# The last mixing of a four-stream layer: which engine multiplies and adds tile 4, and in which order the output is stored

## The chip, the cores and the metric

The kernel runs on one core of a Trainium2 chip. The metric is the device time of one execution in microseconds. The core has five engines with instruction queues of their own: TensorE (PE in the profile), VectorE (DVE), ScalarE (ACT), GpSimd (POOL) and SyncE (SP), which issues the DMAs of interest here.

## The reference

The whole program is a stack of four layers, each a gated cross attention and a gated feed-forward block on x of shape 4 x 256 x 512 (1024 rows of 512 numbers). The change is in the very last step, the end of the fourth feed-forward block. There a row is seen as four streams of 128 numbers, and `hn`, the normalised row, is mixed by a 4 x 4 matrix of that row:

```python
    H_res = sinkhorn_log(H_res_logits)
    H_pre = jax.nn.softmax(H_pre_logits, axis=-1)
    H_post = jax.nn.softmax(H_post_logits, axis=-1)
    H_res = (1.0 - g) * I + g * H_res
    x_pre = jnp.einsum('btnc,btn->btc', x_streams, H_pre)
    y = x_pre @ W_branch
    x_mixed = jnp.einsum('btij,btjc->btic', H_res, x_streams)
    y_distributed = jnp.einsum('btc,btn->btnc', y, H_post)
    return (x_mixed + y_distributed).reshape(B, T, nC)
```

The block's result, times tanh of a gate, is added to x, and x is the output. The kernel has put the gate into the weights, so that the last step is: X[stream i] += sum over j of H[i, j] * hn[stream j], for every row.

## The kernel before, in words

The 1024 rows are 8 tiles of 128 rows (one row per partition). X lies in SBUF as 8 tiles of 128 x 512, `hn_of(7, t)` is tile t of the normalised rows (in the buffer AR), and H (K3, also in AR) holds 16 weights per row.

Each engine has its program written out by hand, in order, and waits on semaphores (`F3[...]`). The end runs as follows.

- GpSimd (`pool_f3`) forms x_pre, and then spreads y over the streams: for each of the eight tiles one 128x512 multiply into a temporary (`PTMP`) and one 128x512 add into X (`add_spread`, L2465 and L2468). Then it raises "posted". It has nothing more to do.
- VectorE (`dve_f3`) runs the balancing of the matrices in 24 and then 25 linear steps of small operations (L2668, L2675, L2679) that read the kernel matrices KP and KT from PSUM. Then come three small operations that finish H (L2697, L2700, L2704), and "mixed" is raised.
- The mixing itself is split three ways. Tiles 0 to 3: VectorE does 16 multiply-adds of 128x128 per tile (L2718), 64 in all, in two halves (tiles 0 and 1, tiles 2 and 3); within a half the streams j are the outer loop, with a drain between them. After each half it raises "done".
- Tiles 4 to 7: products are written to the buffer R16, and TensorE sums X and the four products of a tile in a PSUM bank with an identity matrix as weights (L2511 for X, L2517 for products). ScalarE copies the bank back to X (L2560) and raises "done_act". The products of tiles 5, 6 and 7 are made by ScalarE, 16 activations of 128x128 per tile (L2566). Those of tile 4 are made by VectorE, four operations of 128x512 (L2708), ahead of its multiply-adds.
- SyncE stores one tile per DMA of 256 KB (L2753) in the order 4, 5, 0, 1, 6, 7, 2, 3. Before each it waits for the semaphore of its tile, and it issues nothing past a wait that isn't met. Then it waits for all stores, and the program ends.

Of the kernel before, what the change touches and what calls it, by code (L numbers as in the profile page):

```python
# [9 lines left out]
ALU = mybir.AluOpType  # L10
# [3 lines left out]
P = 128  # L14
B, S, D = 4, 256, 512
SK = 64
T = B * S // P
# [18 lines left out]
NS = 4  # L36
# [21 lines left out]
def build(nc, x_d, ctxT_d, ctxB_d, gx_d, gf_d, wkv_d, w0q_d, w3q_d, wo_d, w4_d, sc4_d, ze4_d, l1wqv_d, l1kr_d, l1o_d,  # L58
# [3 lines left out]
    with ctx:  # L62
# [10 lines left out]
        X = sb("X", [P, T, D])  # L73
# [15 lines left out]
        rms = sb("rms", [P, T])  # L89
# [22 lines left out]
        def bank(i, n=1):  # L112
            return PS[:, i, :] if n == 1 else PS[:, i:i + n, :].rearrange("p a b -> p (a b)")
# [10 lines left out]
        class Sems:  # L124
# [5 lines left out]
            def __getitem__(self, n):  # L130
# [10 lines left out]
        A2 = Sems("a2", "k_in q_in b_in k_mm keys_ready m_mm turned_copied s_mm shifted exps probs t_mm "  # L141
                        "pt_ready mm acc")
        F2 = Sems("f2", "in0 in1 scaled t_mm whi wlo g_mm u_mm silu act ahi alo mm acc")
        F3 = Sems("f3", "w_in rms gate_exp lg_mm to_act from_act pre preT_mm preT y_mm y_sb post posted mixed prod prod_act "
                        "sum_mm done done_act scaled_half")


# [6 lines left out]
        def hn_of(n, t):  # L154
            if n == 7:
                return AR[:, t * D:(t + 1) * D]
            return HN[:, t % 2, :]
# [1193 lines left out]
        def pe_logits(pe, t):  # L1351
            pe.wait_ge(hi_ready, T * 7 + t + 1)
            if t == 0:
                pe.wait_ge(F3["w_in"], 32)
                pe.wait_ge(A3["piece_lo"], 2 * NU0)
# [1077 lines left out]
        NM = NS * NS  # L2433
        LG = at3(4096, T * NL)
        Z = at3(4352, T * NM)
        K3 = at3(4480, T * NM)
# [10 lines left out]
        PTMP = at3(7424, D)  # L2447
# [2 lines left out]
        KT = bank(6)[:, T * NM:2 * T * NM]  # L2450
        TH = T // 2
        T_DVE = 4
        PE_TILES = range(T_DVE, T)

        def products(t, j):
            at = 4096 + (t - T_DVE) * NS * D + j * D
            return R16[:, at:at + D]

        def pool_f3(pool):
            pool_norm(pool, 7)  # L2460
            tmp = PTMP.rearrange("p (i c) -> p i c", i=NS)

            def add_spread(t, src, weights):

                nc.gpsimd.tensor_tensor(tmp, src.unsqueeze(1).to_broadcast([P, NS, P]),  # L2465
                                        weights.unsqueeze(2).to_broadcast([P, NS, P]), ALU.mult)
                pool.drain()
                nc.gpsimd.tensor_tensor(X[:, t, :], X[:, t, :], PTMP, ALU.add)  # L2468
            pool.wait_ge(F3["post"], 1)
            P3 = PP.rearrange("p (t n) -> p t n", t=T)  # L2470

            H4 = AR[:, 0:T * D].rearrange("p (t n c) -> p t n c", t=T, n=NS)
            for n in range(NS):
                dst = XP if n == 0 else XTMP
                nc.gpsimd.tensor_tensor(dst.rearrange("p (t c) -> p t c", t=T), H4[:, :, n, :],
                                        P3[:, :, n].unsqueeze(2).to_broadcast([P, T, P]), ALU.mult)
                pool.drain()
                if n:
                    nc.gpsimd.tensor_tensor(XP, XP, XTMP, ALU.add)
                    pool.drain()  # L2480
            pool.drain().then_inc(F3["pre"], 1)
            nc.gpsimd.tensor_tensor(PP, PP, tg[:, 1, 3:4].to_broadcast([P, T * 2 * NS]), ALU.mult)
            pool.drain()
            pool.wait_ge(F3["y_sb"], 1)
            for t in range(T):
                add_spread(t, Y[:, t * P:(t + 1) * P], P3[:, t, NS:2 * NS])
                pool.drain()
            pool.drain().then_inc(F3["posted"], 1)

        def pe_f3(pe):  # L2490
            for c in range(C):
                i = nc.tensor.matmul(bank(4)[:, 0:NL], ones[:], W24[:, c * NL:(c + 1) * NL], start=c == 0, stop=c == C - 1)
            i.then_inc(F3["lg_mm"], 1)
            pe_logits(pe, 3)
            pe_turn7(pe, 6)
            pe_logits(pe, 4)
            pe_turn7(pe, 7)
            for t in range(5, T):
                pe_logits(pe, t)
            pe.wait_ge(F3["pre"], 1)  # L2500
            for t in range(T):
                i = nc.tensor.transpose(bank(2, 2)[:, t * P:(t + 1) * P], XP[:, t * P:(t + 1) * P], ident[:])
            i.then_inc(F3["preT_mm"], 1)
            pe.wait_ge(F3["preT"], 1)
            for t in range(T):
                i = nc.tensor.matmul(bank(4, 2)[:, t * P:(t + 1) * P], PT[:, t * P:(t + 1) * P], WB,
                                     start=True, stop=True)
            i.then_inc(F3["y_mm"], 1)
            pe.wait_ge(F3["posted"], 1)
            for k, t in enumerate(PE_TILES):  # L2510
                nc.tensor.matmul(bank(k), ident[:], X[:, t, :], start=True, stop=False)  # L2511
                for j in range(NS):
                    if k == 0:
                        pe.wait_ge(F3["prod"], j + 1)
                    else:
                        pe.wait_ge(F3["prod_act"], NS * (k - 1) + j + 1)
                    i = nc.tensor.matmul(bank(k), ident[:], products(t, j), start=False, stop=j == NS - 1)  # L2517
                i.then_inc(F3["sum_mm"], 1)

        def act_f3(act):  # L2520
            act_norm(act, 7, (6, 7))
            asked = [0]

            def asked_for():
                asked[0] += 1
                act.wait_ge(F3["to_act"], asked[0])

            def run(out, in_, f):
                nc.scalar.activation(out, in_, f).then_inc(F3["from_act"], 1)

            def kernel_matrices():
                Z4 = Z.rearrange("p (t i j) -> p t i j", t=T, i=NS)
                run(KP, Z, ACT.Exp)
                run(KT.rearrange("p (t j i) -> p t j i", t=T, j=NS), Z4.rearrange("p t i j -> p t j i"), ACT.Exp)
            asked_for()
            run(K3, Z, ACT.Exp)
            asked_for()
            run(PP, PP, ACT.Exp)
            asked_for()
            run(MX[:, 0:T * NS], MX[:, 0:T * NS], ACT.Ln)  # L2540
            asked_for()
            run(K3, Z, ACT.Exp)
            asked_for()
            run(MX[:, 0:T * NS], MX[:, 0:T * NS], ACT.Ln)
            asked_for()
            kernel_matrices()
            act.wait_ge(F3["preT_mm"], 1)
            nc.scalar.copy(PT[:], bank(2, 2)).then_inc(F3["preT"], 1)
            act.wait_ge(F3["y_mm"], 1)
            nc.scalar.copy(Y, bank(4, 2)).then_inc(F3["y_sb"], 1)  # L2550
            asked_for()
            run(AR[:, 4800:4864], AR[:, 4800:4864], ACT.Ln)
            asked_for()
            kernel_matrices()
            act.wait_ge(F3["mixed"], 1)
            H3 = K3.rearrange("p (t n) -> p t n", t=T)

            def mixed_tile(k):
                act.wait_ge(F3["sum_mm"], k + 1)
                nc.scalar.copy(X[:, T_DVE + k, :], bank(k)).then_inc(F3["done_act"], 1)  # L2560
            for k, t in enumerate(PE_TILES):
                if k == 0:
                    continue
                for j in range(NS):
                    for i_ in range(NS):
                        i = nc.scalar.activation(products(t, j)[:, i_ * P:(i_ + 1) * P],  # L2566
                                                 hn_of(7, t)[:, j * P:(j + 1) * P], ACT.Copy,
                                                 scale=H3[:, t, i_ * NS + j:i_ * NS + j + 1])
                    i.then_inc(F3["prod_act"], 1)
                mixed_tile(k - 1)  # L2570
            mixed_tile(len(PE_TILES) - 1)

        def dve_f3(dve):
# [128 lines left out]
            H3 = K3.rearrange("p (t n) -> p t n", t=T)  # L2702
            diag = H3[:, :, 0:NM:NS + 1]
            nc.vector.tensor_scalar(diag, diag, SG[:, 2:3], None, ALU.add)  # L2704
            dve.drain().then_inc(F3["mixed"], 1)
            t = PE_TILES[0]
            for j in range(NS):
                nc.vector.tensor_tensor(products(t, j).rearrange("p (i c) -> p i c", i=NS),  # L2708
                                        hn_of(7, t)[:, j * P:(j + 1) * P].unsqueeze(1).to_broadcast([P, NS, P]),
                                        H3[:, t, j:NM:NS].unsqueeze(2).to_broadcast([P, NS, P]), ALU.mult)\  # L2710
                    .then_inc(F3["prod"], 1)
            dve.wait_ge(F3["posted"], 1)
            for t0 in range(0, T_DVE, 2):
                for j in range(NS):
# [13 lines left out]
        def _(sp):  # L2728
# [16 lines left out]
            sp_f1(sp)  # L2745
            sp_f2(sp)
            sp_x3(sp)
            for t in (4, 5, 0, 1, 6, 7, 2, 3):
                if t < T_DVE:
                    sp.wait_ge(F3["done"], t // 2 + 1)  # L2750
                else:
                    sp.wait_ge(F3["done_act"], t - T_DVE + 1)
                sp.dma_start(out_d[t * P:(t + 1) * P, :], X[:, t, :]).then_inc(out_stored, 16)  # L2753
            sp.wait_ge(out_stored, 16 * T)

# [149 lines left out]
```

## Time and profile before

| | before |
|---|---|
| median of 3 runs | 1484.44 us (1483.86 to 1485.25) |
| span of the profiled execution | 1484.5 us |
| instructions | 18579 |
| PE busy | 1327.8 us (89%) |
| DVE busy | 1157.6 us (78%) |
| ACT busy | 720.5 us (49%) |
| POOL busy | 337.5 us (23%) |
| DMA, moved | 127.73 MB, mean 86 GB/s |

The profile is of one execution. Busy time is the time in which an engine runs an instruction; the share is of the whole span and says nothing of one stage. The profiled execution's own time is its span, 1484.5 us, which is the median of the runs to within 0.1 us. The mixing is in the last 25 us of it.

### The profile page before, as it was taken

How to read it: one execution, taken by the hardware profiler on the slowest of the kernel's cores; microseconds unless marked ns; L12 is line 12 of the kernel's file. 1: busy time of each engine (PE TensorE's matmuls, PEld its weight loads, DVE VectorE, ACT ScalarE, POOL GpSimd, SP SyncE). 2: the span in 40 equal slices, each digit the busy share in tenths (PEclk: the TensorE clock that was granted, in tenths of full speed). 3: DMA queues.
4: the chain of work that ended last, by engine and by line, in shares of the span. 5: the costliest groups of instructions: out<-in, count | busy, mean ns of one | idle time of the engine just before them, and what ended most of it. 6: DMA issues, size and time to landing. Idle time of an engine off the chain costs nothing.

```text
span 1484.5 us, 18579 instructions
## 1 busy us (share of the span) xinstructions
PE 1327.8 (89%) x6364; PEld 982.2 (66%) x6364; DVE 1157.6 (78%) x2109; ACT 720.5 (49%) x1517; POOL 337.5 (23%) x386
## 2 busy tenths in 40 slices
PE   7999999999998989978999998999999999998104
PEld 5665566566586558746888876777777777777102
DVE  4788988898888997976555567677677677777998
ACT  4777777787523443433222235555464555553104
POOL 1112112121255020143111022221321212212620
PEclk9999999999999999988999998999999999998557
DMA  5678987798820011243211310210101101000001
GB/s 221 168 176 179 246 216 173 191 243 201 214 76 1 1 57 35 51 94 80 72 43 42 105 64 1 72 42 30 71 3 70 72 0 72 1 1 1 1 0 57
DMA packets 37910, 127.73 MB, mean 86 GB/s; under 512 B 4944, under 2 KB 10960, under 8 KB 31680
## 3 DMA queue, kind: packets, MB, share of 16 engines
q1 hardware_dynamic: 26304, 83.38, 16.1%
q0 software_dynamic: 11520, 43.26, 15.4%
q8 instruction: 47, 0.77, 0.2%
q14 instruction: 39, 0.32, 0.1%
HBM read 72.63 MB, written 10.75 MB: 56 GB/s over the span
## 4 chain that ended last, share of the span: by engine, by line
PE 51%; DVE 25%; ACT 7%; DVEq 6%; issue 4%; DMA 4%; POOL 1%; POOLq 0%; SPq 0%
PE PS L150 10%; PE PS L152 10%; PE PS L151 10%; DVE AR L676 4%; PE PS L939 4%; PE PS L976 3%; DMA AR<-AR 3%; ACT s_sb L606 2%; DVE AR L2679 2%; DVE AR L2668 2%; DVE AR L2675 2%; DVEq L666 2%; PE PS L962 1%; DVE AR L682 1%; PE PS L535 1%
## 5 line engine op out<-in xcount | busy, mean ns | idle before, releaser
L438 POOL DMA_DIRECT2D AR<-AR x76 | 74.5, 1094 | 327.4 <-DMA AR<-AR 132.9
L1242 DVE TENSOR_TENSOR R16r<-PS,R16r 64x512 fp32r<-64x512 f32 x128 | 88.1, 689 | 56.7 <-ACT R16r L1097 55.8
L151 PE MATMUL PS<-R16r 128*128 128x512 f32 (+1 forms) x328 | 122.0, 372 | 0.0
L535 PE MATMUL PS<-R,PT 128*128 128x512 f32 x256 | 116.1, 596 | 3.6 <-DVE X L716 3.6
L152 PE MATMUL PS<-R16r 128*128 128x512 f32 (+1 forms) x312 | 119.1, 382 | 0.0
L510 PE MATMUL PS<-R,HT 128*128 128x256 f32 x512 | 116.5, 381 | 2.3 <-ACT R L595 2.0
L510 PEld LDWEIGHTS PS<-R,HT 128*128 128x128 f32 x512 | 94.8, 190 | 15.3 <-ACT R L595 3.7
L606 ACT ACTIVATE s_sb<-PS,sm 128x64 f32<-128x64 f32 x256 | 77.9, 336 | 52.7 <-DVE sm L701 52.2
L1097 ACT CAST R16r<-PS 64x512 fp32r<-64x512 f32 x128 | 74.3, 580 | 49.8 <-PE PS L939 49.0
L1102 ACT COPY AR<-PS 128x512 f32<-128x512 f32 x64 | 37.5, 585 | 124.2 <-PE PS L152 124.2
L150 PE MATMUL PS<-HTr,R16r 128*128 128x512 f32 (+1 forms) x240 | 90.9, 379 | 4.2 <-DVE R16r L190 2.7
L150 PE MATMUL PS<-R16r,HTr 128*128 128x512 f32 (+1 forms) x224 | 91.4, 408 | 0.0
L152 PE MATMUL PS<-HTr,R16r 128*128 128x512 f32 (+1 forms) x240 | 87.6, 365 | 0.0
L535 PEld LDWEIGHTS PS<-R,PT 128*128 128x128 f32 x256 | 47.7, 190 | 57.8 <-issue 54.6
L151 PE MATMUL PS<-R16r,HTr 128*128 128x512 f32 (+1 forms) x224 | 83.9, 375 | 0.0
L676 DVE SCALAR_TENSOR_TENSOR AR<-AR 128x2112 f32<-128x2112 bf16 x28 | 66.1, 2359 | 14.9 <-ACT AR L583 12.1
L2381 DVE TENSOR_TENSOR s_sb<-PS,s_sb 128x1024 f32<-128x1024 f32 x11 | 13.5, 1224 | 81.9 <-PE PS L152 81.9
L976 PEld LDWEIGHTS PS<-kT,AR 128*128 128x128 f32 x512 | 63.8, 196 | 15.4 <-issue 15.4
L151 PEld LDWEIGHTS PS<-R16r 128*128 128x128 f32 x328 | 62.8, 192 | 9.3 <-issue 0.8
L150 PE MATMUL PS<-R16r,PTr 128*128 128x512 f32 x128 | 63.7, 498 | 3.2 <-DVE PTr L1237 3.2
L152 PEld LDWEIGHTS PS<-R16r 128*128 128x128 f32 x312 | 58.5, 188 | 11.9
L2338 ACT CAST R16r<-PS 128x512 fp32r<-128x512 f32 x33 | 24.7, 752 | 85.9 <-PE PS L2252 85.9
(321 smaller groups left out, 3562.4 us busy)
## 6 DMA issues: line engine op xcount, KB each, us to landing
AR<-AR POOLq DMA_DIRECT2D x76, 528.0 KB, 6.8
OR<-in_wo SPq DMA_DIRECT2D x12, 1024.0 KB, 12.1
dequantised<-AR SPq DMA_DIRECT2D x8, 1056.0 KB, 5.5
WR<-in_w0q SPq DMA_DIRECT2D x8, 1024.0 KB, 11.5
AR<-in_w3q SPq DMA_DIRECT2D x8, 1024.0 KB, 7.0
WR<-dequantised SPq DMA_DIRECT2D x22, 256.0 KB, 2.7
AR<-in_nf SPq DMA_DIRECT2D x4, 1056.0 KB, 9.4
nf_in<-in_nf SPq DMA_DIRECT2D x4, 1056.0 KB, 10.7
```

The source lines that it names most:

```text
L150: nc.tensor.matmul(out, ah, bh, start=first, stop=False)
L151: nc.tensor.matmul(out, ah, bl, start=False, stop=False)
L152: return nc.tensor.matmul(out, al, bh, start=False, stop=last_)
L438: nc.gpsimd.dma_start(nf_below(g)[:, part], what[:, part], accum_op=ALU.add, max_dma_last_dim=4 * N_NF // 2).then_inc(added, 16)
L510: i = nc.tensor.matmul(bank(2 + u % 2)[:, tt * 256:(tt + 1) * 256], HT0[:, c, tok], m[:, :, c * B + b, :], start=c == 0, stop=c == C - 1)
L535: i = nc.tensor.matmul(bank(5 + tt), PT[:, at:at + P], vo[:, pr, b, :], start=pr == 0, stop=pr == 1)
L606: i = nc.scalar.activation(s_slot(u)[:, cols], bank(2 + u % 2)[:, cols], ACT.Exp, bias=stat_slot(1, u)[:, j:j + 1], accum_out=stat_slot(2, ...
L676: nc.vector.scalar_tensor_tensor(nf_above, nf_far(g, NLOW + k), rise, nf_above, ALU.min, ALU.subtract if k == 1 else ALU.add).then_inc(A0[ ...
L939: nc.tensor.matmul(o, v[:, 2 * bp * SK:2 * (bp + 1) * SK], wo3(g)[:, h * D:(h + 1) * D], start=True, stop=True).then_inc(A3["piece_mm"], 1)
L976: i = nc.tensor.matmul(bank(3)[:, col:col + SK], QT3[:, at:at + P], kT[:, b * SK:(b + 1) * SK], start=True, stop=True)
L1097: i = nc.scalar.copy(VOh[rows, h // 2, b, :], bank(7)[rows])
L1242: i = nc.vector.tensor_tensor(VOl[rows, h // 2, b, :], bank(7)[rows], VOh[rows, h // 2, b, :].bitcast(F32), ALU.subtract)
```

## The change

Tile 4 leaves the product path. GpSimd, after "posted" and "mixed", multiplies and adds it itself: for each stream j one 128x512 multiply into `PTMP` and one 128x512 add into X, and then raises "posted" a second time. VectorE makes no products and goes from "mixed" to its multiply-adds. TensorE sums three tiles (5, 6, 7), whose products ScalarE makes as before; ScalarE now makes the products of tiles 5 and 6 before its first copy. The stores are issued in the order 5, 0, 1, 4, 6, 2, 3, 7.

```diff
-        PE_TILES = range(T_DVE, T)
+        POOL_TILE = T_DVE
+        PE_TILES = range(T_DVE + 1, T)
 
         def products(t, j):
-            at = 4096 + (t - T_DVE) * NS * D + j * D
+            at = 4096 + (t - PE_TILES[0]) * NS * D + j * D
             return R16[:, at:at + D]
@@ pool_f3, behind the spreading
+                pool.drain()
+            pool.drain().then_inc(F3["posted"], 1)
+            pool.wait_ge(F3["mixed"], 1)
+            t = POOL_TILE
+            for j in range(NS):
+                nc.gpsimd.tensor_tensor(tmp, hn_of(7, t)[:, j * P:(j + 1) * P].unsqueeze(1).to_broadcast([P, NS, P]),
+                                        K3.rearrange("p (t n) -> p t n", t=T)[:, t, j:NM:NS].unsqueeze(2)
+                                        .to_broadcast([P, NS, P]), ALU.mult)
+                pool.drain()
+                nc.gpsimd.tensor_tensor(X[:, t, :], X[:, t, :], PTMP, ALU.add)
                 pool.drain()
             pool.drain().then_inc(F3["posted"], 1)
@@ pe_f3
-                    if k == 0:
-                        pe.wait_ge(F3["prod"], j + 1)
-                    else:
-                        pe.wait_ge(F3["prod_act"], NS * (k - 1) + j + 1)
+                    pe.wait_ge(F3["prod_act"], NS * k + j + 1)
@@ act_f3
             def mixed_tile(k):
                 act.wait_ge(F3["sum_mm"], k + 1)
-                nc.scalar.copy(X[:, T_DVE + k, :], bank(k)).then_inc(F3["done_act"], 1)
+                nc.scalar.copy(X[:, PE_TILES[k], :], bank(k)).then_inc(F3["done_act"], 1)
             for k, t in enumerate(PE_TILES):
-                if k == 0:
-                    continue
                 for j in range(NS):
@@
-                mixed_tile(k - 1)
+                if k:
+                    mixed_tile(k - 1)
             mixed_tile(len(PE_TILES) - 1)
@@ dve_f3, behind "mixed"
-            t = PE_TILES[0]
-            for j in range(NS):
-                nc.vector.tensor_tensor(products(t, j).rearrange("p (i c) -> p i c", i=NS),
-                                        hn_of(7, t)[:, j * P:(j + 1) * P].unsqueeze(1).to_broadcast([P, NS, P]),
-                                        H3[:, t, j:NM:NS].unsqueeze(2).to_broadcast([P, NS, P]), ALU.mult)\
-                    .then_inc(F3["prod"], 1)
             dve.wait_ge(F3["posted"], 1)
@@ the stores
-            for t in (4, 5, 0, 1, 6, 7, 2, 3):
+            for t in (5, 0, 1, POOL_TILE, 6, 2, 3, 7):
                 if t < T_DVE:
                     sp.wait_ge(F3["done"], t // 2 + 1)
+                elif t == POOL_TILE:
+                    sp.wait_ge(F3["posted"], 2)
                 else:
-                    sp.wait_ge(F3["done_act"], t - T_DVE + 1)
+                    sp.wait_ge(F3["done_act"], t - PE_TILES[0] + 1)
```

## Rows read from the trace of the kernel before

**Rows 1.** The chain that ended last: start us, us, what; its last compute piece.

```profile
1479.74 1.58 DVE X L2718 x6
```

**Rows 2.** Timeline of the mixing: start, us, engine, line, operation, count [idle before].

```profile
1460.78 4.78 ACT L2566 ACTIVATE R<-AR 128x128 f32<-128x128 f32 x16 [41.38 <-DVEq L2705]
1460.83 2.50 DVE L2708 TENSOR_TENSOR R<-AR 128x512 f32<-128x512 f32 x4
...
1463.25 18.06 DVE L2718 SCALAR_TENSOR_TENSOR X<-AR,X 128x128 f32<-128x128 f32 x64
...
1467.31 4.78 ACT L2566 ACTIVATE R<-AR 128x128 f32<-128x128 f32 x16
...
1472.46 4.78 ACT L2566 ACTIVATE R<-AR 128x128 f32<-128x128 f32 x16
...
1479.70 0.58 ACT L2560 COPY X<-PS 128x512 f32<-128x512 f32 x1 [1.99 <-PE PS L2517]
```

**Rows 3.** Span; SP's last issues; time to landing: at 1481.37, 1481.74, 1473.3 and 1473.7.

```profile
span 1484.5 us, 18579 instructions
...
1481.37 0.33 SPq L2753 DMA_DIRECT2D out<-X  x1
1481.74 0.43 SPq L2753 DMA_DIRECT2D out<-X  x1
...
out<-X SPq DMA_DIRECT2D x1, 256.0 KB, 2.0
...
out<-X SPq DMA_DIRECT2D x1, 256.0 KB, 2.3
...
out<-X SPq DMA_DIRECT2D x2, 256.0 KB, 2.7
```

**Rows 4.** Timeline: spreading beside VectorE, and the same VectorE form undisturbed.

```profile
1416.18 1.04 POOL L2465 TENSOR_TENSOR AR<-AR 128x512 f32<-128x512 f32 x1
...
1416.78 0.59 DVE L2686 TENSOR_TENSOR AR<-AR 128x128 f32<-128x128 f32 x1 [0.42 <-ACT AR L2529]
1417.37 1.26 POOL L2468 TENSOR_TENSOR X<-X,AR 128x512 f32<-128x512 f32 x1
1417.45 1.33 DVE L2688 TENSOR_TENSOR AR<-AR 128x128 f32<-128x128 f32 x1
1418.77 1.04 POOL L2465 TENSOR_TENSOR AR<-AR 128x512 f32<-128x512 f32 x1
...
1460.09 0.29 DVE L2700 TENSOR_TENSOR AR<-AR 128x128 f32<-128x128 f32 x1
```

**Rows 5.** Timeline at 454 to 462 us: L206 alone and beside GpSimd; line L1484: ns min/median/max.

```profile
454.06 0.69 DVE L206 TENSOR_TENSOR HN<-HN,lnw 128x512 f32<-128x512 f32 x1
...
458.62 2.68 POOL L1484 TENSOR_TENSOR AR<-R,hm 128x512 f32<-128x512 f32 x2
...
459.01 1.38 DVE L206 TENSOR_TENSOR HN<-HN,lnw 128x512 f32<-128x512 f32 x1
...
L1484 POOL TENSOR_TENSOR AR<-R,hm x16: 1033/1039/1581, 433.6 to 462.4; 128x512 f32<-128x512 f32 x16
```

**Rows 6.** Timeline at 619 and 638 us: one GpSimd form in two places.

```profile
619.57 2.43 POOL L237 TENSOR_SCALAR veps<-mv 128x2 f32<-128x2 f32 x1 [21.86 <-DVE mv L177]
619.57 2.36 DVE L676 SCALAR_TENSOR_TENSOR AR<-AR 128x2112 f32<-128x2112 bf16 x1
...
638.49 0.22 POOL L237 TENSOR_SCALAR veps<-mv 128x2 f32<-128x2 f32 x1 [3.19 <-DVE mv L177]
```

**Rows 7.** Line L2668, the balancing's operation on PSUM: ns min/median/max, starts.

```profile
L2668 DVE TENSOR_TENSOR AR<-PS,AR x196: 210/212/225, 1377.8 to 1458.8; 128x64 f32<-128x64 f32 x196
```

**Rows 8.** Timeline at 903 us: a narrow GpSimd operation and a wide one of VectorE.

```profile
902.98 1.64 POOL L886 TENSOR_TENSOR sm<-sm,half 128x8 f32<-128x8 f32 x1
...
903.25 0.69 DVE L1226 TENSOR_TENSOR s_sb<-s_sb,AR 128x512 f32<-128x512 f32 x1
```

**Rows 9.** Busy us by engine in stretches of the mixing; PEclk is the granted clock.

```profile
1460.80:1464.50 3.70, 2.92 (x4) 1.37 (x5) 3.67 (x9) 3.70 (x13) 0.00 (x0) 0.50 0.01 2
1464.50:1481.40 16.90, 15.17 (x36) 6.40 (x34) 16.25 (x60) 12.53 (x40) 0.00 (x0) 1.00 0.22 84
```

More of the change, by code:

```diff
@@ L143, in build @@
         F2 = Sems("f2", "in0 in1 scaled t_mm whi wlo g_mm u_mm silu act ahi alo mm acc")
-        F3 = Sems("f3", "w_in rms gate_exp lg_mm to_act from_act pre preT_mm preT y_mm y_sb post posted mixed prod prod_act "
+        F3 = Sems("f3", "w_in rms gate_exp lg_mm to_act from_act pre preT_mm preT y_mm y_sb post posted mixed prod_act "
                         "sum_mm done done_act scaled_half")
```

## The prediction

> **What bounds the kernel now.** I read the last 25 us only, because the diff touches nothing earlier. First the chain of waits, followed back from the end: its last compute piece is VectorE on X, six multiply-adds in 1.58 us, 0.263 each [rows 1]. Then the timeline of the stretch. VectorE makes the products of tile 4 from 1460.83, starts its 64 multiply-adds (L2718) at 1463.25 and ends them at 1463.25 + 18.06 = 1481.31. ScalarE and TensorE work beside it on tiles 4 to 7; their last copy ends at 1479.70 + 0.58 = 1480.28, so they are 1.0 us ahead of VectorE [rows 2]. Last the stores: two are issued back to back at 1481.37 and 1481.74, the second takes 2.3 us to land, and the execution ends at 1484.5, its span [rows 3]. From VectorE's last multiply-add to the end are 1484.5 - 1481.3 = 3.2 us. The profiled span (1484.5) is as good as the median of the runs (1484.44), so changes to the one are added to the other.
>
> **Removed: tile 4's four products on VectorE.** The multiply-adds start where the products started: 1463.25 - 1460.83 = 2.42 us earlier [rows 2]. Their other condition, the first "posted", is long met: GpSimd is done with the spreading at about 1421, and 40 us of VectorE's balancing come behind it [rows 4]. Alone this puts VectorE's end at 1478.89.
>
> **ScalarE and TensorE: three tiles in place of four.** ScalarE makes three sets of products as before, but its first copy no longer stands between the first two. A set takes 4.78, a set with a copy 1472.46 - 1467.31 = 5.15 [rows 2]. New, from 1460.78: set of tile 5 to 1465.6, set of tile 6 to 1470.3, copy 5 and set of tile 7 to 1475.5, copy 6; TensorE adds the last product in about 1 us, and copy 7 ends near 1477.2. TensorE's part is smaller than before (15 sums for 20). That is 1.7 us ahead of VectorE even in the best case, so it costs and saves nothing. The cover would be gone only if TensorE stayed slow, a rival below.
>
> **Added: tile 4 on GpSimd.** Per stream j one 128x512 multiply and one 128x512 add, the same two operations with the same operand shapes as the spreading (L2465, L2468): 1.04 and 1.26 us, start to start with the drains 1.18 and 1.40 [rows 4]. Four times 2.58 is 10.3 us, so undisturbed GpSimd would run from 1460.9 to 1471.2, and only the store of tile 4 waits for it: nothing is queued behind it. By itself it is hidden behind 18 us of VectorE.
>
> **What it does to VectorE is the main term.** The 64 multiply-adds read two tiles in SBUF (AR and X), and GpSimd's eight operations read SBUF too. The trace has such meetings. L2686 and L2688 are VectorE operations with both inputs in SBUF; undisturbed, the same form takes 0.29 (L2700). Beside the spreading they took 0.59 and 1.33, and both ended 0.15 us after the GpSimd operation they met (1417.22 to 1417.37, 1418.63 to 1418.78), while GpSimd's 1.04 and 1.26 were not stretched [rows 4]. So VectorE stood still until GpSimd's operation was over: 1.04 us lost on the 1.26 us add. The reverse holds as well. L206 normally takes 0.69; in a stretch where both engines had work queued back to back it took 1.38, and the GpSimd operations beside it 2.68 for two overlapping ones, instead of 1.04 each (the median of the line): they took turns. GpSimd's second one ended at 461.30, 0.91 behind L206's end at 460.39, so some 0.13 of its 1.04 had been spent ahead [rows 5]. The very kind of instruction at stake, SCALAR_TENSOR_TENSOR on two SBUF tiles, is in it: a small GpSimd operation on L237 lasted 2.43 us, as long as L676 beside it (2.36), against 0.22 where it started just ahead of such a one [rows 6]. What covers the 24 us of spreading today is that the balancing reads one input from PSUM: its operations stay at 212 ns, at most 225, beside GpSimd or not [rows 7]. A bound from below: a VectorE operation with two SBUF inputs lost nothing beside a tiny GpSimd operation of 1.64 us [rows 8]. There the tile read is 8 elements wide, so the reading itself is short; the new operations are 512 wide like the ones that held.
>
> Size of the term. A GpSimd operation gets in when the current multiply-add is through, and then holds VectorE for about 0.90 (multiply) or 1.12 (add), its own time less the 0.14 spent ahead. VectorE's next one ends 0.15 behind it, instead of 0.26 behind its predecessor. The loss of a multiply is then 0.90 + 0.15 - 0.26 = 0.79 at least, and 1.04 - 0.15 = 0.89 where GpSimd starts with the port free; of an add 1.01 and 1.11. Four times 1.80 is 7.2, four times 2.00 is 8.0; I take 7.7. Ends for the range: nothing lost (0) and, with 0.15 us more at each of eight switches, 9.2 + 1.2 = 10.4.
>
> The Trainium skill ("SBUF — State Buffer", section "Who interferes with whom") has a rule for this: a VectorE instruction with two SBUF inputs and a GpSimd instruction that reads SBUF exclude each other, and the later one is fully blocked for the whole of the other. Charged with whole instructions the term would be 4 x (1.04 + 1.26) = 9.2 us and the time 1491.9. The rows above show that part of the start-up is overlapped, so my sum stays at 7.7. That VectorE stands still, by that rule, the trace agrees (1.33 us for 0.29).
>
> **Stores.** SP takes them as 5, 0, 1, 4, 6, 2, 3, 7. It stands at tile 0 until VectorE's first half is done; behind it wait 1, 4 and 6, all needed early enough: VectorE's second half lasts 9 us more and a store about 2. But tile 7, ready at 1477, is now behind 2 and 3, so three stores follow VectorE's end, not two. The two at the end today, 0.37 apart at issue, land 2.0 and 2.3 us after it; the last two of the three at 1473, 2.7 us (median of the two) [rows 3]. So a store behind others waits for their transfers: the second lands 0.37 + 2.3 = 2.7 us after the first issue, 0.7 behind the first, and the third should be another 0.7 behind. Bounds 0.37 and 0.7; I take 0.68.
>
> **Sum.** 1484.44 - 2.42 + 7.7 + 0.68 = 1490.4: VectorE ends at 1486.6, 3.85 us before the end. 6 us or 0.4% slower. Nothing hides the loss: ScalarE and TensorE finish 9 us earlier.
>
> **Rivals.**
> 1. VectorE is not held (its short multiply-adds pass through between GpSimd's accesses). For it: the small-operation case [rows 8]; no row has 64 short ones in a stream. Against it: [rows 4, 5, 6]. Time 1484.44 - 2.42 + 0.68 = 1482.7, 0.12% less. This decides from a loss under 1.7 us: then the kernel is not slower. Chance 0.14.
> 2. Held for a part of each operation only, half say: a loss of 3 to 5 us, 1485.7 to 1487.7. The two rows that ended exactly 0.15 behind GpSimd speak against it. Chance 0.07.
> 3. GpSimd is starved by the stream and gets in only at VectorE's drains (64 at 0.263 are 16.8 us of the 18.06, so a drain adds 0.17). The loss is then 4 x (0.90 - 0.17) + 4 x (1.12 - 0.17) = 6.7, the time 1489.4, and GpSimd would be spread over the whole 25 us and end just before VectorE. Against it: GpSimd got its turn after each VectorE operation [rows 5]. Chance 0.10.
> 4. TensorE stays at half clock. It is granted 0.50 until 1464.5, after its long idle time, and 1.00 from there [rows 9]; that is its 1.2 and then its 2.4 GHz. Now ScalarE's products come each 4.78/4 = 1.20 us, but at half clock a product costs 1.46 to 1.7 us (four records, two products, in 2.92 to 3.4 us), so TensorE is as busy as before at the start and should rise as before. If not, 14 further sums from 1461.9 take 20.4 to 24 us, and ScalarE ends at 1483 to 1486.7, about with VectorE at most. It would decide only together with rival 1, where VectorE isn't held: then tile 7's store sets the end and the time is 1486 to 1489. Chance 0.03.
>
> **How the numbers follow.** Forecast 0.66, rivals 0.14, 0.07, 0.10, 0.03. The forecast's own range is 1489.0 to 1492.0. For 8 in 10 I go up to 1492.5 (most of the upper end of the hold) and down to 1486.0, through rival 3 and most of rival 2, leaving rival 1 out. A measurement of this kernel tells about 0.2%, 3.0 us. Slower than 1487.4: forecast, rival 3, most of 4 and a third of 2, 0.80. Within: rival 1, the rest of 2, 0.17. Faster than 1481.5 would need 1.2 us more than the whole gain: 0.03.
>
> **What would show it.** In the profile after: L2718's successor starts near 1460.8; in its first 11 us it loses about 7.7 us, so that the 64 take 25.8 us from first to last in place of 18.06, with some eight of them 1.0 to 1.4 us long instead of 0.35; GpSimd's eight operations keep 1.04 and 1.26 or are stretched by up to 0.3; they end near 1472. ScalarE's last copy ends near 1477. The last store issued is tile 7's, third behind VectorE's end, landing 3.4 us behind the first of them. If no multiply-add is above 0.4 us while GpSimd runs, the main term is wrong and rival 1 is right; if GpSimd's operations stand only at multiples of eight multiply-adds, rival 3.

## The result, and the profile after

| | before | after |
|---|---|---|
| median (6 runs each) | 1484.85 us (1483.86 to 1487.92) | 1490.89 us (1489.35 to 1492.51) |
| ratio to before | 1 | 1.0036, 95% interval 1.0025 to 1.0048 |
| span of the profiled execution | 1484.5 us | 1489.4 us |
| "mixed" to the end of the span | 23.6 us | 29.0 us |

The change made the kernel slower by 0.36%, 5.3 us (the ratio times 1484.85; the two medians alone differ by 6.0). The last row takes away what the two executions did before the mixing: "mixed" (the start of VectorE's first instruction behind it) came at 1460.83 before and at 1460.42 after, a difference that the change did not make; from there to the end are 1484.5 - 1460.8 = 23.6 and 1489.4 - 1460.4 = 29.0. The steps below use this measure, since it is steadier than the time of a run. Over the six kernels below "mixed" moved between 1458.4 and 1461.5 us, though four of them have no edit ahead of it (e4 and e6 have four copies on ScalarE there).

The timeline of the mixing in the kernel after, which answers to [rows 2] (start, us, engine, line, operation, count):

```profile
1460.37 9.46 ACT L2572 ACTIVATE R<-AR 128x128 f32<-128x128 f32 x32 [41.49 <-DVEq L2712]
1460.41 1.05 POOL L2493 TENSOR_TENSOR AR<-AR 128x512 f32<-128x512 f32 x1 [39.72 <-DVEq L2712]
1460.42 25.19 DVE L2719 SCALAR_TENSOR_TENSOR X<-AR,X 128x128 f32<-128x128 f32 x64
1461.60 1.40 POOL L2497 TENSOR_TENSOR X<-X,AR 128x512 f32<-128x512 f32 x1
...
1463.14 1.17 POOL L2493 TENSOR_TENSOR AR<-AR 128x512 f32<-128x512 f32 x1
1464.46 1.39 POOL L2497 TENSOR_TENSOR X<-X,AR 128x512 f32<-128x512 f32 x1
...
1477.02 0.58 ACT L2568 COPY X<-PS 128x512 f32<-128x512 f32 x1 [1.57 <-PE PS L2525]
```

The row to see is the third: the same 64 multiply-adds as before, 25.19 us from first to last in place of 18.06. The loss is 7.13 us. Narrow windows of VectorE's timeline show where it sits. Four of the eight long multiply-adds of the kernel after, the ones beside the four GpSimd rows above:

```profile
1460.42 1.19 DVE L2719 SCALAR_TENSOR_TENSOR X<-AR,X 128x128 f32<-128x128 f32 x1
...
1461.79 1.35 DVE L2719 SCALAR_TENSOR_TENSOR X<-AR,X 128x128 f32<-128x128 f32 x1
...
1463.33 1.13 DVE L2719 SCALAR_TENSOR_TENSOR X<-AR,X 128x128 f32<-128x128 f32 x1
...
1464.65 1.35 DVE L2719 SCALAR_TENSOR_TENSOR X<-AR,X 128x128 f32<-128x128 f32 x1
```

Read with the GpSimd rows they are a zip. GpSimd's multiply runs from 1460.41 to 1461.46, and VectorE's first multiply-add ends at 1461.61, 0.15 behind it. One short multiply-add passes. The add runs to 1463.00, and the multiply-add started at 1461.79 ends at 1463.15, again 0.15 behind. All eight meetings (a GpSimd operation beside a long multiply-add) look so. Against the undisturbed 0.34 us the eight are longer by 0.85, 1.01, 0.79, 1.01, 0.64, 1.02, 0.79 and 1.02 us, which makes 7.13, the whole loss. The 0.64 is the one that met a drain: GpSimd's third multiply began at 1465.99 beside the last multiply-add of a stream, and VectorE, which drains between two streams, started its next multiply-add only at 1466.34. Since the eight make up the whole loss, nothing else was stretched; the line's own row has its median still at 344 ns (ns min/median/max):

```profile
L2719 DVE SCALAR_TENSOR_TENSOR X<-AR,X x64: 339/344/1358, 1460.4 to 1485.3; 128x128 f32<-128x128 f32 x64
```

The last three stores of the kernel after, with their times to landing, answer to [rows 3]:

```profile
1485.66 0.33 SPq L2756 DMA_DIRECT2D out<-X  x1
1486.04 0.43 SPq L2756 DMA_DIRECT2D out<-X  x1
1486.51 0.45 SPq L2756 DMA_DIRECT2D out<-X  x1
...
out<-X SPq DMA_DIRECT2D x1, 256.0 KB, 2.0
...
out<-X SPq DMA_DIRECT2D x1, 256.0 KB, 2.3
...
out<-X SPq DMA_DIRECT2D x1, 256.0 KB, 2.5
```

Tile 7's store is third behind VectorE's end (1485.61). It lands at 1486.51 + 2.5 = 1489.0, and the span ends 3.84 us after VectorE, before 3.15.

### The profile page after: what moved, and what is told of

Same layout as the page of the kernel before. It is cut to its first block, busy times and chain, and to the rows that moved or that the text cites. A ratio compares the mean times of both kernels' runs of the same rounds, so it can differ in the third digit from the quotient of the medians.

```text
span 1489.4 us, 18571 instructions
## 1 busy us (share of the span) xinstructions
PE 1323.5 (89%) x6354; PEld 978.9 (66%) x6354; DVE 1162.0 (78%) x2105; ACT 719.8 (48%) x1516; POOL 347.9 (23%) x394
## 4 chain that ended last, share of the span: by engine, by line
PE 51%; DVE 26%; DVEq 6%; ACT 6%; issue 4%; DMA 4%; POOL 1%; POOLq 0%; SPq 0%
PE PS L150 10%; PE PS L152 10%; PE PS L151 10%; DVE AR L676 5%; PE PS L939 4%; PE PS L976 3%; DMA AR<-AR 3%; DVE AR L2686 2%; ACT s_sb L606 2%; DVE AR L2675 2%; DVE AR L2682 2%; DVEq L666 2%; DVE X L2719 2%; PE PS L962 1%; DVE AR L682 1%
```

## The experiments

The theory: each GpSimd operation that reads SBUF stops each VectorE operation with two SBUF inputs for as long as it runs. The rivals: the time was lost elsewhere; any access of GpSimd stops VectorE; the loss has a fixed part; the store order is hidden. All kernels start from the kernel after. e1, e2, e3 and e5 change one thing in it, e4 one on VectorE's side, e6 goes on from e4. Each kernel has one profile. In the fences L-numbers differ with each kernel; the diffs are shortened (`...`, the names of new semaphores, and in e6 the narrower copies to PSUM); the multiply-adds are the SCALAR_TENSOR_TENSOR rows.

### e1: without GpSimd's tile

```diff
-            for j in range(NS):
-                nc.gpsimd.tensor_tensor(tmp, hn_of(7, t)..., ALU.mult)
-                pool.drain()
-                nc.gpsimd.tensor_tensor(X[:, t, :], X[:, t, :], PTMP, ALU.add)
-                pool.drain()
```

> The kernel after, with GpSimd's eight operations on tile 4 left out (tile 4 is stored unmixed). Theory (GpSimd's reads of SBUF stop VectorE): the 64 multiply-adds take 18.1 us from first to last, not 25.2, no multiply-add is longer than 0.36 us, and the end comes 7.1 us before that of the kernel after: ratio to before 0.9989 (1484.85 - 2.4 + 0.7 = 1483.1). Rival (the time was lost elsewhere, say in a slower stretch ahead of the mixing or in the instruction stream of the changed program): the multiply-adds get back to 18.1 us, but the time stays above 1487.

Ratio to before 0.9989 (0.9980 to 0.9998). The multiply-adds on VectorE's timeline, from "mixed" on:

```profile
1461.52 18.07 DVE L2712 SCALAR_TENSOR_TENSOR X<-AR,X 128x128 f32<-128x128 f32 x64
```

They are back at the time of before, and "mixed" to the end is 1483.4 - 1461.5 = 21.9 us, 7.1 less than with GpSimd's tile. The whole loss hangs on the eight operations; besides them only the order of the stores cost time. It also shows the other two terms alone: 21.9 against 23.6 is -1.7 us, which is the 2.42 us of removed products less about 0.7 us for the stores.

### e2: GpSimd writes and reads nothing

```diff
-            for j in range(NS):
-                nc.gpsimd.tensor_tensor(tmp, hn_of(7, t)..., ALU.mult)
-                pool.drain()
-                nc.gpsimd.tensor_tensor(X[:, t, :], X[:, t, :], PTMP, ALU.add)
+            for j in range(10):
+                nc.gpsimd.memset(XTMP, 0.0)
+                pool.drain()
```

> The kernel after, with GpSimd's eight operations replaced by ten fills of 128x1024 in SBUF with drains (about 1.0 us each from the trace of before, 128x1024 MEMSET 0.96 us; tile 4 is stored unmixed). They write SBUF and read nothing. Theory (it is the second read interface that both want): VectorE isn't stopped, the 64 multiply-adds take 18.1 to 18.5 us, ratio to before 0.999. Rival A (any access of GpSimd to SBUF stops VectorE): about ten multiply-adds of 1.0 to 1.2 us, 26 us in all, ratio 1.004. Rival B (GpSimd stops VectorE only at its start): a few tenths lost per fill, 20 to 22 us.

Ratio to before 0.9985 (0.9975 to 0.9995). Groups of instructions by line in the mixing (count | busy us, mean ns of one | idle us before):

```profile
L2715 DVE SCALAR_TENSOR_TENSOR X<-AR,X 128x128 f32<-128x128 f32 x64 | 17.5, 345 | 0.7
...
L2493 POOL MEMSET AR<- 128x1024 f32 x10 | 9.5, 951 | 40.8 <-DVEq L2708 39.7
```

The multiply-adds' line (ns min/median/max):

```profile
L2715 DVE SCALAR_TENSOR_TENSOR X<-AR,X x64: 342/344/352, 1458.4 to 1476.2; 128x128 f32<-128x128 f32 x64
```

GpSimd was busy for 9.5 us beside VectorE, nearly as long as in the kernel after (eight operations, 10.2 us), and no multiply-add was longer than 0.35 us. GpSimd's fills stayed at 951 ns. So it isn't the writing, nor GpSimd being at work. What the fills lack is the reading and the arithmetic; e4 will show that the arithmetic alone holds nothing up. The Trainium skill ("SBUF — State Buffer", "Who interferes with whom") says that a VectorE instruction with two SBUF inputs collides with a GpSimd one that reads SBUF and not with one that only writes it; this run agrees, with 0 of 64 against 8 of 64.

### e3: tile 7 stored ahead of tiles 2 and 3

```diff
-            for t in (5, 0, 1, POOL_TILE, 6, 2, 3, 7):
+            for t in (5, 0, 1, POOL_TILE, 6, 7, 2, 3):
```

> The kernel after with one edit: tile 7 is stored ahead of tiles 2 and 3, as before. Theory: the third store behind VectorE's end costs 0.68 us; from the end of the last multiply-add to the end of the span are 3.2 us in place of 3.8, the multiply-adds stay at 25.2 us. Rival (each transfer is hidden, the tail is one landing): 3.8 us stay.

One run (1489.51 us), so there is no ratio. The multiply-adds and the span:

```profile
span 1487.8 us, 18571 instructions
...
1459.44 25.19 DVE L2719 SCALAR_TENSOR_TENSOR X<-AR,X 128x128 f32<-128x128 f32 x64
```

VectorE ends at 1484.63 and the span 3.15 us later, as before the change (3.15) and not 3.84. The order of the last three stores is worth 0.69 us by itself, 0.68 in the sum. The other kernels bear it out: with tile 7 third behind VectorE the tail is 3.84 us in e1 and 3.83 in e2, e4 and e5.

### e4: the accumulators of VectorE in PSUM

```diff
+        ACCS = (3, 4, 5, 7)
@@ act_f3, ahead of the wait for "mixed"
+            act.wait_ge(F3["posted"], 1)
+            for t in range(T_DVE):
+                i = nc.scalar.copy(bank(ACCS[t]), X[:, t, :])
+            i.then_inc(F3["accs"], 1)
@@ dve_f3, with a wait for "accs" ahead of the loops
-                            xt = X[:, t, i_ * P:(i_ + 1) * P]
-                            nc.vector.scalar_tensor_tensor(xt, hn_of(7, t)...
+                            xt = bank(ACCS[t])[:, i_ * P:(i_ + 1) * P]
+                            to = xt if j < NS - 1 else X[:, t, i_ * P:(i_ + 1) * P]
+                            nc.vector.scalar_tensor_tensor(to, hn_of(7, t)...
```

> The kernel after, in which ScalarE copies tiles 0 to 3 of X into four PSUM banks right behind the spreading (about 1421 to 1424 us, in 40 us of idle time), and VectorE's multiply-adds accumulate in PSUM, the last stream writing to X in SBUF. Each multiply-add has then one input in SBUF and one in PSUM; GpSimd does tile 4 as in the kernel after. Theory: like the balancing's operations on PSUM, they aren't stopped: no multiply-add above 0.4 us, 18.1 to 18.5 us in all (L2697, the same form with a PSUM input, takes 0.35), GpSimd's operations back at 1.04 and 1.26, ratio to before 0.999. Rival (the weights, a pointer into SBUF, or the write to SBUF is what collides): 22 to 25 us, ratio 1.002 to 1.004.

Ratio to before 0.9984 (0.9975 to 0.9993). VectorE's and GpSimd's groups in the mixing:

```profile
L2726 DVE SCALAR_TENSOR_TENSOR PS<-AR,PS 128x128 f32<-128x128 f32 x48 | 13.0, 350 | 0.6 <-issue 0.2
L2498 POOL TENSOR_TENSOR X<-X,AR 128x512 f32<-128x512 f32 x4 | 5.1, 1271 | 0.6
L2726 DVE SCALAR_TENSOR_TENSOR X<-AR,PS 128x128 f32<-128x128 f32 x16 | 4.3, 341 | 0.1
L2494 POOL TENSOR_TENSOR AR<-AR 128x512 f32<-128x512 f32 x4 | 4.2, 1048 | 40.2 <-DVEq L2717 39.7
```

The line of the 48 (ns min/median/max), and two rows of the timelines in the stretch in which both were at work:

```profile
L2726 DVE SCALAR_TENSOR_TENSOR PS<-AR,PS x48: 347/350/357, 1459.8 to 1475.1; 128x128 f32<-128x128 f32 x48
...
1466.11 1.28 POOL L2498 TENSOR_TENSOR X<-X,AR 128x512 f32<-128x512 f32 x1
...
1466.52 2.16 DVE L2726 SCALAR_TENSOR_TENSOR X<-AR,PS 128x128 f32<-128x128 f32 x8
```

The same work on both engines at the same time, and neither waits: multiply-adds at 350 and 341 ns, GpSimd at 1.05 and 1.27 us, where the kernel after has it at 1.17 and 1.40. The 64 go from 1459.80 to 1477.66, 17.86 us, 0.2 under the lower end expected, for which I have no reason. No multiply-add was above 0.36 us. From "mixed" to the end are 21.7 us, 1.9 less than before the change. The weight, which is read from SBUF through a pointer, does not collide. Nor does the write to SBUF of the last stream: of its 16 multiply-adds eight ran beside GpSimd, the second row above, at 0.34 us as well. Both engines still read the buffer AR, so sharing a buffer isn't the cause either. One edit, which moves one of two inputs out of SBUF, turns the change into a gain. (In 48 of the 64 the output moved too; it is the eight that show that the input alone does it. Two inputs in SBUF with the output in PSUM was not run.)

### e5: half of GpSimd's tile

```diff
-            for j in range(NS):
+            for j in range(2):
```

> The kernel after, with GpSimd doing only the streams j = 0 and 1 of tile 4: four operations in place of eight (half of tile 4's mixing is left out). Theory (each GpSimd operation that reads SBUF costs VectorE a fixed wait, whatever stands around it): four long multiply-adds, the sum of their excess is half of the 7.13 us, 3.5 to 3.6, and the 64 take 21.6 us; from mixed to the end 25.5 us. Rival (the loss has a fixed part, a start of GpSimd or a slow first meeting): well off the half, under 3.0 or above 4.2 us.

One run (1486.47 us), so there is no ratio. The multiply-adds:

```profile
1459.17 21.72 DVE L2719 SCALAR_TENSOR_TENSOR X<-AR,X 128x128 f32<-128x128 f32 x64
```

21.72 - 18.06 = 3.66 us, four long multiply-adds of 1.19, 1.35, 1.13 and 1.35 us, the same as the first four of the kernel after (0.85 + 1.01 + 0.79 + 1.01 = 3.66). That is 0.06 above the upper end that was expected, because the half that is left doesn't have the cheap meeting at a drain. "Mixed" to the end is 25.6 us. The loss goes by the meeting and has no fixed part.

### e6: more work for GpSimd, once it is free of charge

Built on e4, and shown against it.

```diff
+        def dve_streams(t):
+            return NS if t < T_DVE - 1 else NS - 2
@@ pool_f3, behind tile 4
+            t, h = T_DVE - 1, NS - 2
+            for j in range(NS):
+                nc.gpsimd.tensor_tensor(tmp[:, h:, :], ..., ALU.mult)
+                pool.drain()
+                nc.gpsimd.tensor_tensor(X[:, t, h * P:D], X[:, t, h * P:D], PTMP[:, h * P:D], ALU.add)
+                pool.drain()
+            pool.drain().then_inc(F3["posted"], 1)
@@ dve_f3
-                        for i_ in range(NS):
+                        for i_ in range(dve_streams(t)):
@@ the stores
+                    if dve_streams(t) < NS:
+                        sp.wait_ge(F3["posted"], 3)
```

> Built on the kernel with accumulators in PSUM. GpSimd does, besides tile 4, the output streams 2 and 3 of tile 3 (four multiplies and four adds of 128x256, an estimate of 1.45 us per pair with the drains by half the 128x512 ones), so VectorE has 56 multiply-adds. Theory (nothing is stopped, so work moves to GpSimd at its own price): VectorE ends 15.6 us after mixed, GpSimd 16.1, ScalarE's last copy 17.1 and sets the end; from mixed to the end 19.5 us in place of 21.7; ratio to before 0.997. Rival (ScalarE's longer lead doesn't matter, the stores do: four of them within 1.5 us wait for one another's transfers): 20.2 to 20.8 us, ratio 0.9977. If the PSUM form were stopped after all by the narrower operations, VectorE would end above 18 us and nothing is gained.

Ratio to before 0.9978 (0.9968 to 0.9988). The last groups of VectorE, GpSimd and SyncE on the timeline:

```profile
1475.35 1.64 DVE L2739 SCALAR_TENSOR_TENSOR X<-AR,PS 128x128 f32<-128x128 f32 x6
...
1476.53 0.62 POOL L2506 TENSOR_TENSOR AR<-AR 128x256 f32<-128x256 f32 x1
1477.28 0.72 POOL L2510 TENSOR_TENSOR X<-X,AR 128x256 f32<-128x256 f32 x1
...
1476.18 2.82 SPq L2778 DMA_DIRECT2D out<-X  x4
```

From VectorE's start (1461.19) to the end are 20.1 us: better than e4 by 1.6, but 0.6 short of the 19.5 of the theory and just under the rival's 20.2 to 20.8. VectorE came near (15.8 for 15.6). GpSimd wasn't: a pair of 128x256 operations takes 1.63 us from start to start, not the 1.45 that I had estimated from the wide ones, so it ends 16.9 us after "mixed" and not 16.1. Tile 3's store waits for it and, with tile 7's, makes two stores at the very end: 16.9 and a tail of 3.2 us are the 20.1, where the expected 19.5 was 17.1 and a tail of 2.4. All three ends now lie within 1.2 us, so little is left to move. Of all kernels here this has the shortest time from "mixed" to the end; the ratios alone would not part it from e4, since their intervals overlap. 0.9978 against 1.0036 is 0.6% better than the kernel after (the quotient of two ratios, not one comparison).

## Why the prediction was right

Direction and mechanism held, and the time: 1490.4 forecast, 1490.89 measured, ratio 1.0036 for a forecast 1.0040. That the two times lie within 0.5 us is in part luck. The sum forecast 6.0 us more; from "mixed" to the end it was 5.4, and "mixed" alone moves by 3 us from kernel to kernel. Point by point:

- Products removed, -2.42 us: the first multiply-add starts where the products did, 1460.42 beside ScalarE's 1460.37. Shown by e1 together with the stores.
- The hold, +7.7 us (7.2 to 8.0): 7.13 measured, just under the lower end. The step that is off is the share of meetings with the port free: I had put it at over half. The rows say that in six of eight meetings GpSimd came in while a multiply-add was running, and these cost the lower price: 0.79 for a multiply and 1.01 to 1.02 for an add, as worked out. Only the first multiply found nothing running on VectorE (0.85), and the third multiply met a drain (0.64).
- Turns: as forecast, GpSimd was served after every multiply-add at hand, and rival 3 (starved until the drains) is out: its operations start 1.2 to 1.6 us apart. They were stretched by 0.13 us each, but for the first.
- Stores, +0.68: 3.84 - 3.15 = 0.69 between the profiles, 0.69 by e3.
- ScalarE and TensorE: the last copy ends at 1477.6, forecast 1477.2. It did not set the end; it was 8.0 us ahead of VectorE, forecast 9. But one reason given was wrong, that TensorE's clock would rise as before; see below. It did rise, at 1467.8, so rival 4 is out.
- The stated equality of span and median was wrong. The time of a run is 1.7 to 2.2 us more than its span in every run for which both are at hand, so the profiled execution of before must itself have taken 1486.2 to 1486.7 us (an estimate, 1484.5 and that difference), above the median of 1484.85. It did no harm since only differences were used.

Rival 1 (not held) is refuted by the eight long rows, rival 2 (held in part) by their ends 0.15 behind GpSimd and by 7.13 us where it had 3 to 5. From "mixed": 23.6 - 2.4 + 7.1 + 0.7 = 29.0 us, which is what the profile after has.

## What to carry to other kernels

Before giving GpSimd elementwise work "beside" VectorE, look at the operands: if VectorE's instructions have two tiles in SBUF and GpSimd reads SBUF, the two take turns, and VectorE pays for most of what GpSimd takes over (here 7.1 us for 10.2 us of GpSimd, to save 2.4 us). How small a GpSimd operation may be before this ends was not tested; the one with 8 elements per partition cost VectorE nothing [rows 8]. Look in the trace for one VectorE row of a kind that is longer beside GpSimd than elsewhere; two such rows were enough here. With one input in PSUM the overlap was real (e4), and an idle ScalarE could put it there.

## What I had not expected of the hardware

TensorE's clock rose later than before, though TensorE was as busy. Stretches of the kernel after (PE busy (x), PEld, DVE, ACT, POOL, granted clock, DMA share, GB/s), to be set beside [rows 9]:

```profile
1460.40:1464.50 4.10, 2.80 (x4) 1.20 (x5) 4.08 (x6) 4.10 (x15) 3.66 (x4) 0.50 0.00 0
1464.50:1468.00 3.50, 3.50 (x6) 1.46 (x5) 3.42 (x6) 3.50 (x14) 3.22 (x3) 0.53 0.02 5
1468.00:1477.00 9.00, 8.98 (x21) 3.61 (x19) 8.74 (x24) 7.45 (x25) 3.29 (x3) 1.00 0.08 29
```

Before, TensorE began at 1461.58, was busy without a break and had 1.00 (2.4 GHz) from about 1464.7. After, it began at 1461.70, was as busy (without a break from there to 1464.5: 2.80 us in the first row, 2.92 in [rows 9]) and had 0.50 (1.2 GHz) up to about 1467.8: 3.1 us more at the lower clock. The rows in which it rose, before and after:

```profile
1464.60:1464.70 0.10, 0.10 (x1) 0.03 (x1) 0.10 (x2) 0.10 (x2) 0.00 (x0) 0.71 0.00 0
...
1467.70:1467.80 0.10, 0.10 (x1) 0.00 (x0) 0.10 (x1) 0.10 (x2) 0.10 (x1) 0.68 0.00 0
```

In a kernel where TensorE sets this end that would be visible; here VectorE's end was 8 us later and hid it. It has nothing to do with the hold: in e1, where VectorE is not held, "mixed" came at 1461.5 and the clock was 0.50 until 1468, then 0.93:

```profile
1467.00:1468.00 1.00, 1.00 (x2) 0.34 (x1) 1.00 (x5) 1.00 (x5) 0.00 (x0) 0.50 0.00 0
1468.00:1470.00 2.00, 2.00 (x6) 0.97 (x5) 1.93 (x8) 2.00 (x9) 0.00 (x0) 0.93 0.00 0
```

From TensorE's first product to the rise it was 3.1 us before, and 5.5 to 6.1 us in the kernel after and the six experiments. The kernels differ in the source of the first products, VectorE's four within 2.5 us before and ScalarE's four within 4.8 after. But up to 1464.5 TensorE's own rows hardly show it, so it is not shown to be the cause, and there is one execution before to set against seven; the cause stays open. ScalarE's last copy ends 16.9 to 17.2 us behind "mixed" in all kernels with three tiles on TensorE.
